# Biases of the experts applied through the gates, and the attention's sums laid out by value channel

## What is computed

```python
# layer 0
xn = layernorm(x)
x  = x + attn0(xn) @ Wo.T + moe(xn)

# attn0: linear and causal, 16 heads of 8 channels; q and k turned by RoPE, then elu(.) + 1
K_sum = K_sum + k_t
KV    = KV + k_t[:, None] * v_t[None, :]       # 8 x 8 sums per head
y_t   = (q_t @ KV) / max(q_t . K_sum, 1e-6)

# moe: 8 experts, 2 for each token
selected   = gate_probs * expert_mask / (sum of both + 1e-8)
h          = gelu(x @ W1[e] + b1[e])
expert_out = h @ W2[e] + b2[e]
out        = sum over e of expert_out * selected[e]

# layer 1
xn = layernorm(x)
x  = x + (attn1(xn) @ w_proj + b_proj) + ffn1(xn)
```

## Time and profile before

| | |
|---|---|
| times | 354.26, 354.57, 354.77 us, median 354.57 us |
| profiled execution | 354.33 us, its span from first to last instruction 352.5 us |
| PE busy | 339.4 us, 96% of the span; weight loads 296.4 us |
| DVE busy | 320.9 us, 91% |
| ACT busy | 271.4 us, 77% |
| POOL busy | 208.8 us, 59% |
| mean granted clock of TensorE | 0.995 of full speed |

### The profile page before, as it was taken

One profiled execution on the slowest core, in us unless ns is written; L12 is line 12 of the kernel. 1 busy time (PEld: TensorE's weight loads), 2 busy tenths in 40 slices (PEclk: granted clock), 3 DMA queues, 4 the chain that ended last, 5 costly groups with the idle time before them and its releaser, 6 DMA issues.

```text
span 352.5 us, 9136 instructions
## 1 busy us (share of the span) xinstructions
PE 339.4 (96%) x2488; PEld 296.4 (84%) x2488; DVE 320.9 (91%) x633; ACT 271.4 (77%) x764; POOL 208.8 (59%) x229
## 2 busy tenths in 40 slices
PE   8999878999999999999999999999999899999995
PEld 3888334799999999999999899999998688778875
DVE  5999999899999999998899899998978799998665
ACT  2997946968887878787787678778985987777751
POOL 3899202843323666766776678778877278884110
PEclk9999989999999999999999999999999999999999
DMA  5896196454444555555555654565452002221112
GB/s 161 238 278 181 32 387 240 114 147 131 136 130 137 156 152 149 159 150 156 155 157 154 168 155 133 164 186 145 120 141 75 9 7 54 60 63 30 30 32 60
DMA packets 45520, 46.98 MB, mean 133 GB/s; under 512 B 6928, under 2 KB 33712, under 8 KB 45216
## 3 DMA queue, kind: packets, MB, share of 16 engines
q1 hardware_dynamic: 40432, 37.17, 35.7%
q0 software_dynamic: 4320, 8.86, 10.1%
q10 hardware_dynamic: 720, 0.38, 0.5%
HBM read 32.88 MB, written 13.50 MB: 132 GB/s over the span
## 4 chain that ended last, share of the span: by engine, by line
PE 86%; DVE 9%; DMA 2%; issue 2%; POOL 0%; ACT 0%; DVEq 0%; POOLq 0%
PE banks L574 18%; PE banks L561 18%; PE banks L700 7%; PE banks L701 7%; PE banks L364 4%; PE banks L1012 3%; PE banks L545 3%; PE banks L1041 2%; PE banks L1088 2%; PE banks L352 2%; PE banks L1070 2%; PE banks L1050 2%; PE banks L776 2%; PE banks L1022 2%; PE banks L1058 2%; PE banks L320 2%
## 5 line engine op out<-in xcount | busy, mean ns | idle before, releaser
L489 POOL DMA_INDIRECT xg<-xn_rows,slot_tok x71 | 76.5, 1077 | 77.0 <-PE banks L545 43.6
L591 ACT ACTIVATE xT<-banks,b1T 128x128 f32<-128x128 f32 x284 | 81.5, 375 | 18.8 <-PE banks L561 18.6
L506 POOL DMA_INDIRECT qk_exp<-expert_rows,ranki x64 | 74.0, 1156 | 19.1 <-issue 18.7
L574 PE MATMUL banks<-w_sb,xT 128*128 x568 | 78.9, 282 | 0.0
L561 PE MATMUL banks<-xgT,w 128*128 128x128 f32 x568 | 75.4, 276 | 0.0
L574 PEld LDWEIGHTS banks<-w_sb,xT 128*128 128x128 f32 x568 | 69.3, 192 | 0.5
L561 PEld LDWEIGHTS banks<-xgT,w 128*128 128x128 f32 x568 | 69.0, 192 | 0.8 <-issue 0.5
L712 DVE TENSOR_TENSOR cq<-banks,phi 128x360 f32<-128x360 f32 (+1 forms) x96 | 47.4, 548 | 7.6 <-PE banks L701 6.7
L684 DVE TENSOR_TENSOR low<-outer,high 128x1152 fp32r<-128x1152 f32 x32 | 43.5, 1358 | 3.2 <-ACT high L678 3.2
L721 DVE TENSOR_REDUCE sums<-cq 128x144 f32<-128x1152 f32 x32 | 43.0, 1343 | 0.1
L678 ACT CAST high<-outer 128x1152 fp32r<-128x1152 f32 x32 | 36.9, 1154 | 7.0 <-DVE outer L667 5.7
(11 more groups left out here) (210 smaller groups left out, 691.0 us busy)
## 6 DMA issues: line engine op xcount, KB each, us to landing
w<-in_L_ffn_W SPq DMA_DIRECT2D x71, 256.0 KB
expert_rows<-ye SPq DMA_DIRECT2D x71, 64.0 KB
expert_rows<-x_sb SPq DMA_DIRECT2D x2, 2048.0 KB, 9.7
x_sb<-in_L_attn_x SPq DMA_DIRECT2D x8, 256.0 KB, 4.0
xn_rows<-xn SPq DMA_DIRECT2D x8, 256.0 KB, 2.9
w_sb<-in_L_ffn_W SPq DMA_DIRECT2D x8, 256.0 KB, 3.9
out<-outer SPq DMA_DIRECT2D x7, 256.0 KB, 2.4
xg<-xn_rows,slot_tok POOLq DMA_INDIRECT x71
```

Source lines behind the costliest of these rows:

```text
L489: pool.indirect_dma_start(out=xg[n][:, :], out_offset=None, in_=xn_dram, in_offset=bass.IndirectOffsetOnAxis(ap=slot_tok[:, j:j + 1], axis ...
L506: pool.indirect_dma_start(out=y_moe[:, i, k, :], out_offset=None, in_=y_dram, in_offset=bass.IndirectOffsetOnAxis(ap=ranki[:, 0, k, i:i + ...
L574: last = nc.tensor.matmul(y, hidT[p][:, c, :], w2_sb[:, ds(e * NC + c, 1), :], start=False, stop=(c == NC - 1))
L591: last = nc.scalar.activation(hidT[p][:, c, :], slot_bank(j)[:, c * P:(c + 1) * P], ACT.Gelu_apprx_tanh, bias=b1T[:, ds(e * NC + c, 1)])
```

## The change

The change has two parts, and with them come changes of where and when data is prepared.

1. **Biases.** The matmul of ones in `down` goes, 71 in all. Instead DVE makes a table of gates: for each token and expert the gate, zero where the expert is not chosen (`gate_of_all`, 256 numbers per row). That takes an added `both` and a multiplication in front of `phi(0)`, and another multiplication in `gates`. After tile (0, 1), `split_gates` writes the table as a rounded part and a rest into the space of `xn[2]` and `xn[3]` (2 operations with 1024 elements). At every second sequence PE transposes 128 columns of the table (`attn_transpose`), ACT copies them to `gT`, and `attn_project` ends with one fp32r matmul of 64 rows and 256 columns that multiplies the gates by `bias`. In its rows `bias` holds b2 for each of the four combinations of a tile with a part, and in its last 128 columns b_proj. The bias rows are loaded by 18 DMAs of SP (16 of b2, 2 of b_proj), issued after `mu` and ahead of `save(0)`; ACT makes the rounded part (`bias_high`, 384 elements) and POOL the rest (`bias_parts`, 384 elements). The five operations of `split_biases`, two small loads and the six DMAs of L1304 go. The two matmuls of ones for b_proj in layer 1 become fp32r.

2. **Sums by value channel.** The 16 x 9 x 8 numbers are ordered channel of the value, head, channel of the key, in place of head, channel of the value, channel of the key. The cut into banks is then three times 384 columns, and `attn_apply` is one operation over three banks with 1152 elements in place of three. `attn_sums` writes its 144 results with a stride.

```diff
+    def bias_high(act):
+        act.wait_ge(bias_loaded, 16 * 18)
+        nc.scalar.activation(bias_high_of, bias_raw, ACT.Copy, scale=const("low_row")).then_inc(bias_ready, 1)
+    def bias_parts(pool):
+        pool.wait_ge(bias_ready, 1)
+        nc.gpsimd.tensor_tensor(bias[:, :], bias_raw, bias_high_of.bitcast(f32), ALU.subtract).then_inc(bias_ready, 1)
...
         y = slot_bank(j)[:, 0:D]
-        nc.tensor.matmul(y, ones_bf[:, :], bias3[:, ds(e * D, D)], start=True, stop=False)
         for c in range(NC):
             last = nc.tensor.matmul(y, hidT[p][:, c, :], w2_sb[:, ds(e * NC + c, 1), :],
-                                    start=False, stop=(c == NC - 1))
+                                    start=(c == 0), stop=(c == NC - 1))
...
-        for n, (lo, hi) in enumerate(HEADS):
-            last = nc.vector.tensor_tensor(
-                cq4[:, lo:hi, :, :], ps[n][:, 0:(hi - lo) * E9 * DH].rearrange("p (h e d) -> p h e d", e=E9, d=DH),
-                q[:, lo:hi, :].unsqueeze(2).broadcast_to([P, hi - lo, E9, DH]), ALU.mult)
-        last.then_inc(cq_ready, 1)
+        cum = ps_all[:, 0:NBANK * 512].rearrange("p (n c) -> p n c", n=NBANK)[:, :, 0:EB * D]
+        nc.vector.tensor_tensor(cq.rearrange("p (n e c) -> p n e c", n=NBANK, c=D),
+                                cum.rearrange("p n (e c) -> p n e c", c=D),
+                                q.unsqueeze(1).unsqueeze(1).broadcast_to([P, NBANK, EB, D]), ALU.mult
+                                ).then_inc(cq_ready, 1)
...
     def attn_transpose(pe, b):
         pe.wait_ge(y_ready, b + 1)
+        if b == 0:
+            pe.wait_ge(gates_split, 1)
+        if b % 2 == 0:
+            nc.tensor.transpose(ps[6][:, 3 * P:4 * P], gate_row[:, b * NGR:(b + 2) * NGR], ident)
...
+        rows = slice(b % 2 * NGR, (b % 2 + 1) * NGR)
+        nc.tensor.matmul(ps[5][:, 0:2 * D], gT[rows, :], bias[rows, 0:2 * D], start=False, stop=True,
+                         skip_group_check=True).then_inc(o_ps, 1)
...
-            sp.dma_start(bias_sp[:, 0:BIASP // P], b2.rearrange("e h -> (e h)").rearrange("(p c) -> p c", p=P)).then_inc(bias_in, 16)
-            sp.dma_start(bias_sp[:, BIASP // P:NBIAS // P], b_proj.rearrange("(p c) -> p c", p=P)).then_inc(bias_in, 16)
             sp.dma_start(mu[:, 0:1], mu_r.rearrange("(p c) -> p c", p=P)).then_inc(bias_in, 16)
             sp.dma_start(mu[:, 1:2], mu_k.rearrange("(p c) -> p c", p=P)).then_inc(bias_in, 16)
+            sp.wait_ge(zeros_ready, 2)
+            for q in range(P // (2 * NE)):
+                for t in range(2):
+                    lo = (2 * q + t) * NE
+                    sp.dma_start(bias_raw[lo:lo + NE, t * D:(t + 1) * D], b2).then_inc(bias_loaded, 16)
+            for lo in (0, 32):
+                sp.dma_start(bias_raw[lo:lo + 1, BIASP:NBIAS], b_proj.rearrange("(a c) -> a c", a=1)
+                             ).then_inc(bias_loaded, 16)
...
+            def split_gates():
+                whole = yT0[:, 0:NT * NE].rearrange("p (b f) -> p b f", b=B).unsqueeze(2).broadcast_to([P, B, 2, 2 * NE])
+                done(nc.vector.tensor_copy(gate_parts[:, :, :, 0, :], whole))
+                TT(gate_parts[:, :, :, 1, :], whole, gate_parts[:, :, :, 0, :].bitcast(f32), ALU.subtract
+                   ).then_inc(gates_split, 1)
...
                     tile(b, r, b % 2)
+                    if b == 0 and r == 1:
+                        split_gates()
```

More of the change, by code:

```diff
@@ L58, in constant_table @@
     put("row_no", row)
+    put("low_row", row // 32 % 2)
     put("rows_in_front", P * row)
@@ L99, in build @@
     NB = 4
-    xn = [sbuf(f"xn{p}", [P, GT, D]) for p in range(NB)]
+    xn_all = sbuf("xn_all", [P, NB, GT, D])
+    xn = [xn_all[:, p, :, :] for p in range(NB)]
     xT = [sbuf(f"xT{p}", [P, GT, P]) for p in range(2)]
@@ L118, in build @@
     bg_sb = sbuf("bg_sb", [P, NE])
-    bias_sp = sbuf("bias_sp", [P, NBIAS // P])
-    bias_rest = sbuf("bias_rest", [P, 2, NBIAS // P])
-    bias_part = sbuf("bias_part", [P, 3, NBIAS // P], bf16)
-    bias3 = sbuf("bias3", [P, NBIAS], bf16)
+    bias = sbuf("bias", [P, NBIAS], f32r)
     ones_bf = sbuf("ones_bf", [P, P], bf16)
@@ L695, in attn_cumsum @@
         parts = [(tri_r, kept(r, p))] + ([(ones_r, kept(0, p))] if r else [])
-        for n, (lo, hi) in enumerate(HEADS):
-            cols = slice(lo * E9 * DH, hi * E9 * DH)
-            o = ps[n][:, 0:(hi - lo) * E9 * DH]
+        for n in range(NBANK):
+            cols = slice(n * EB * D, (n + 1) * EB * D)
+            o = ps[n][:, 0:EB * D]
             for m, (w, at) in enumerate(parts):
@@ L720, in attn_sums @@
             v.wait_ge(y_ready, i // 2)
-        nc.vector.tensor_reduce(sums[:, r, :, :], cq4, AX.X, ALU.add).then_inc(sums_ready, 1)
+        nc.vector.tensor_reduce(sums[:, r, :, :].rearrange("p h e -> p e h"), cq4, AX.X, ALU.add).then_inc(sums_ready, 1)
     def attn_reciprocal(v, b):
@@ L752, in attn_yT @@
             act.wait_ge(o_ps, b)
[L753 removed]
+        if b % 2 == 0:
+            nc.scalar.copy(gT[:, :], ps[6][:, 3 * P:4 * P])
+        nc.scalar.copy(yT0, ps[6][:, P:3 * P]).then_inc(yT_ready, 1)
     def attn_tokens_bank(pe):
@@ L1054, in project2_tensor @@
         pe.wait_ge(tanh_ready, min(g + 2, NG) if isinstance(g, int) else g + 2)
-        nc.tensor.matmul(ps[4], ones_bf[:, :], bias3[:, BIASP:BIASP + D].unsqueeze(1).broadcast_to([P, GT, D]),
+        nc.tensor.matmul(ps[4], ones_r[:, :], bias[:, BIASP:NBIAS].unsqueeze(1).broadcast_to([P, GT, D]),
                          start=True, stop=False, skip_group_check=True)
@@ L1138, in last_tensor @@
         for h in range(2):
-            nc.tensor.matmul(out_half(h), ones_bf[:, :], bias3[:, BIASP:BIASP + D].unsqueeze(1).broadcast_to([P, HALF, D]),
+            nc.tensor.matmul(out_half(h), ones_r[:, :], bias[:, BIASP:NBIAS].unsqueeze(1).broadcast_to([P, HALF, D]),
                              start=True, stop=False, skip_group_check=True)
@@ L1457, in _ @@
                     deviation(pool, 0, g + 5, g + 5)
-            split_biases(pool)
+            bias_parts(pool)
             pool.wait_ge(logits_read, 1)
@@ L1719, in _ @@
                 rope_sum_vector(v, NG - 1, f)
+            both = TT(oh[:, 0, :, :], oh[:, 0, :, :], oh[:, 1, :, :], ALU.add)
+            n_route[0] += 1
+            both.then_inc(route, 1)
             v.wait_ge(gate_exp, 1)
-            done(RED(row(5), masked, AX.X, ALU.add))
+            RED(row(5), masked, AX.X, ALU.add)
+            v.wait_ge(route, n_route[0])
+            done(TT(gate_of_all, masked, oh[:, 0, :, :], ALU.mult))
             def gates():
```

70 lines of the change are left out of this document (31 added, 39 removed).

## The result

The changed kernel takes 366.06 us (364.03 to 367.49), beside the kernel before with 354.69 us (354.26 to 356.19) on the same chip: ratio 1.031, 95% interval 1.027 to 1.035. On another chip, beside the experiments, the ratio was 1.032 (1.028 to 1.035). The forecast was 361.9 us with a range up to 365.5: slower as foretold, but 4 us too little. The profiled execution took 367.49 us, with a span of 365.7 us, 13.2 us more than that of before.

What follows compares the result with a forecast made beforehand. PE was taken to bound the steps, with DVE close behind. From 354.33 us: +7.3 front, +0.7 gates on DVE, +2.9 `split_gates`, -3.5 PE's steps, -0.1 last apply gave 361.6 us profiled, 361.9 us predicted; range 357.2 to 365.5 us.

Steps and rivals of the forecast that it cites:

- the matmuls added: In the steps: 16 matmuls of 256 columns at 0.13 us cost 2.1 us, eight transposes of gates 0.9 us.
- The removed biases: In the steps: 71 bias matmuls fewer save 0.11 us each, 0.07 us behind sums, 6.5 us in all.
- The front: Before the steps: 18 bias loads delay `save(0)`, ACT stalls 7.3 us, and the front's terms sum to +7.3 us.
- rival (a): In the front: short loads issue faster, at 0.3 us; ACT stalls 3.9 us, total 358.4 us; chance 0.12.
- The clock's term: In the front: PE's first work behind ACT's stall runs at half clock, +1.3 us.
- split_gates: At sequence 0: two operations of 1024 elements and a wait take 2.4 us; PE loses 2.9 us waiting.
- Gates on DVE: Ahead of the steps: three operations of 256 numbers take 1.3 us, of which +0.7 us reaches PE.
- The layout: In the steps: one apply saves DVE 0.24 us per sequence, but earns almost nothing, 0.1 us behind the last tile.
- (b): In the front: the loads cost SP almost nothing and `save(0)` lands in time; total 355.1 us; chance 0.05.
- (c): Whole kernel: faster than before, with nearly free loads, a cheap copy and PE gaining 5.8 us; 351.8 us; chance 0.04.
- (e): In the steps: one apply costs as much as three, or strided sums cancel its gain; +0.3 us; no separate chance.
- (d): In the front: loads touching few partitions take SP 0.6 us each; total 364.3 us, or 367 us; chance 0.11.

Runs made afterwards that it cites:

- experiments 2 and 4: Changed kernel with the gates' matmul over 128 rows: 361.32 us, ratio 1.019; changed kernel with that matmul cut into two of 64 rows: 366.51 us, ratio 1.033.
- experiment 3: By number, the changed kernel without the gates' matmul: 357.27 us, ratio 1.007. The changed kernel with the split early is another run: 363.85 us, ratio 1.025.
- experiment 6: Changed kernel with 22 more matmuls of zeros on PE while ACT waits for `save(0)`: 364.23 us, ratio 1.025.
- experiment 7: Kernel before with only the sums by value channel and one apply, its biases as they were: 354.78 us, ratio 0.9995.

## Why the prediction was right in its sign and short in its size

**The step that failed** is "I take 0.13 us, so 16 x 0.13 = 2.1 us", in the part on the matmuls added. It was priced by columns alone, from rows of the form 128*128, and the added one is 64*128. It measured 0.51 us. The change of form costs 0.39 us of that each time (experiments 2 and 4), 15 x 0.39 = 5.9 us in all; the mend was worth 5.8 us (4.5 by the ratios). With it the stretch from the first transposes of y to the last apply is 180.95 us, 3.1 us less than before, close to the forecast's 3.5; without it that stretch is 2.5 us more than before. The stated bound of PE's gain, 2 to 6 us, didn't take it in, since both ends rested on rows of one form; the uncommon 64 rows stood in the diff. With this one term right the sum would have been 361.6 + 5.9 = 367.5 us for the profiled execution, which took 367.5. That it meets so well is luck: the split's stretch came out 1.2 us below its forecast, and 1.4 us in the landing of the last DMA made up for it.

**The removed biases** gave more than 0.07 us behind sums: 0.13 us, the upper end. PE's gain is 8.5 us and not 6.5. In the changed kernel it is spent. Behind the first transposes of y and ahead of the last apply there are 63 of the 71 steps (7.5 us of gain), 15 passages and 7 transposes of gates: -7.5 + 15 x 0.51 + 7 x 0.11 = +0.9 us. Measured it is +2.5 us. The missing 1.6 us do not come from the split, since the same stretch is 186.51 us with the split early (experiment 3) and 186.54 us without. Nor do they come from the passage: with 128 rows the count gives -7.5 + 15 x 0.12 + 0.8 = -4.9 us and the profile -3.1. What takes them is not shown; DVE, with 11.3 to 11.6 us of work in each period, is the nearest suspect there.

**The front** was right in its mechanism and nearly in its sum, by two errors that offset each other. The issues take 0.34 us, nearer to the 0.3 us of rival (a) than to 0.47, so 18 of them are 6.1 us and not 8.5. On the other side SP stood 2.32 us in the issue of Wo in the profiled execution, 1.5 us more than in that of before, where the changed kernel's second profile shows 1.10 us. ACT's wait is 5.31 us in one and 4.78 in the other, against 7.3 forecast, and `slot_tok` comes 7.1 or 5.1 us late. So that +7.07 us met the forecast's +7.3 is luck in part: the second profile is 2 us below it. `save(0)` goes out 1.27 us earlier in the second; the waits differ by 0.5 us only, since ACT itself comes to this point 0.7 us earlier there. The clock's term, 1.3 us, lies within the 1.2 to 2.0 us of experiment 6. `choose` started free of POOL as foretold (second and third operation 0.42 us, before 0.93 and 1.38), and `bias_parts` held up one operation of DVE, as the term of +0.5 us had it:

```profile
41.78 0.42 DVE L1605 TENSOR_TENSOR cq<-outer,r 128x256 f32<-128x256 f32 x1
42.24 0.42 DVE L1606 SCALAR_TENSOR_TENSOR outer<-cq,cst 128x256 f32<-128x256 f32 x1
...
44.52 0.82 DVE L1605 TENSOR_TENSOR outer<-cq,r 128x256 f32<-128x256 f32 x1
...
44.05 1.01 POOL L414 TENSOR_TENSOR bias<-phi,high 128x384 fp32r<-128x384 f32 x1 [3.97 <-ACT high L410]
```

**split_gates** was read wrongly: its two operations have 512 elements each, not 1024, and take 1.1 us together, not 2.4. The wait of PE was 1.94 us, not 2.9. Its price is 2.2 us where PE's clock holds. The mend was worth 3.3 us (2.2 by the ratios), near the forecast's 2.9, but the forecast had left out what can raise it: in some executions PE's clock falls behind the stall.

**Gates on DVE** cost +0.47 us for +0.7. **Layer 1** cost 0, as forecast. **The layout** made apply 1.35 us and left the total unchanged, as forecast, and this is shown by itself (experiment 7). **Rivals:** (b), (c) and (e) fell with the traces: 0.34 us between issues, 5.31 us of waiting for `save(0)`, and 1.35 us for apply. (d) names the right size for the wrong reason.

## What to carry to other kernels

Price a matmul by its form and by that of its neighbours, not by its columns alone: one with 64 rows between others of 128 cost four times what the same product padded with zeros to 128 rows did (0.51 against 0.12 us). Before loads are added to a queue, look for what stands behind them that another engine waits for; moved behind the last load of W2, the same 18 loads held up nothing that the trace shows. And when an engine is relieved, read how near the second one is: with DVE at 11.67 of 11.87 us, 8.5 us taken from PE were worth 5.1.
